# Second cross attention: an item's key scales are issued ahead of its columns and keys

## The chip, the cores and the metric

The kernel runs on one core of a Trainium2 chip. The metric is the device time of one execution in microseconds (us). The engines named here are TensorE (PE in the profile; PEld is its weight load), VectorE (DVE), ScalarE (ACT), GpSimd (POOL) and SyncE (SP), which here only waits and issues DMAs.

## The reference, cut to what matters

The model is two layers of cross attention, self attention and a routed feed-forward part on x of 64 x 32 x 256, with a context of 64 batch items of 257 keys and 128 features. The change lies in the cross attention of the second layer:

```
def _L1_xattn_ref(hidden_states, encoder_hidden_states, Wq, Wk, Wv, Wo, gq, gk):
    q = (hidden_states @ Wq).reshape(B, Sq, H, D)           # H = 16 heads, D = 128
    k = (encoder_hidden_states @ Wk).reshape(B, Skv, H, D)
    v = (encoder_hidden_states @ Wv).reshape(B, Skv, H, D)
    q = rmsnorm(q, gq)
    k = rmsnorm(k, gk)
    scores = jnp.einsum('bqhd,bkhd->bhqk', q, k) * scale
    attn = jax.nn.softmax(scores, axis=-1)
    out = jnp.einsum('bhqk,bkhd->bqhd', attn, v)
    return out.reshape(B, Sq, H * D) @ Wo
```

The key weights are folded into the queries ahead of time, so the scores come straight from the context. What is left of the key's rmsnorm is one factor for each head and key, 1 / rms(k), by which a score is multiplied before the softmax.

## The kernel before, in words

`cross_attention` (from L380) is used for both layers; everything below holds for layer 1, the second. An item is one batch element. `ITERS` = 8 passes handle `NB` = 8 items each; the document counts passes and the items of a pass from 0. An item has 16 heads of 32 queries, that is 512 rows of scores, or R = 4 tiles of 128 rows by 257 keys. So a pass has ST = 32 tiles, 0 to 31, and tile 4b is the first of item b.

For each item three things come from DRAM. The *pair* (L534) holds the item's columns (the context transposed, which the scores read) and its keys (which the mixing reads), in one transfer of 256.5 KB into one of RING = 8 places. The *key scales* (L539) hold the factors 1 / rms(k) for all heads, spread over the partitions that hold a head's 32 queries, in HR = 4 transfers of 128.5 KB into one of SCALES = 4 places; the trace calls them all_big<-rk, as the places lie in a large shared buffer. Nothing else in the item loop is loaded by SyncE, but for the weight codes of the next stage (`load_codes`, L2185) behind items 1 and 3 in passes 0 to 3, and its scales (`load_scales`, L2195) ahead of the last pass. GpSimd gathers rows of the expert output for the next pass by its own DMAs (L1065), 2 to an item in passes 0 to 5, each item's behind the mixing of an earlier one.

The work on a tile s: TensorE computes the scores (`score`, L604 to L614, into one of two PSUM buffers); VectorE multiplies them by the key scales and takes each row's maximum (`weigh`, L857), which frees the PSUM buffer; VectorE makes the shift (L865), ScalarE the exponential (L747), VectorE the division (L881); TensorE turns the tile (`turn`, L620), ScalarE keeps it (L755), and TensorE mixes it with the keys (`mix`, L634). On TensorE a step s of a pass is turn(s), score(s + AHEAD), mix(s - LAG), with AHEAD = 6 and LAG = 3. Behind step 31 come the head of the next pass (query norms L577, queries L600) and the projection (L643), between which the first 6 scores of the next pass stand. All engines work in program order.

Who waits for the loads: the score of an item's first tile waits for the pair (`keys_loaded`), the weighing of its first tile waits for the key scales (`kscale_loaded`). Score s also waits until tile s - 2 is weighed. SyncE waits, ahead of a pair, until the item 8 before it is mixed (`mixed`), and ahead of the key scales until the item 4 before it is weighed (`weighed`). Both counters start with a credit, of RING and of PRE = 12, so that the first places count as free:

```
pe.sem_inc(mixed, RING)
dve.sem_inc(weighed, PRE)
```

SyncE calls `items` for passes 0 to 3, then in a loop for passes 4 to 6, waits for the query norms of the last pass (`n_made`), loads the scales of the next stage, and calls `items` for pass 7.

Of the kernel before, what the change touches and what calls it, by code (L numbers as in the profile page):

```python
# [379 lines left out]
def cross_attention(nc, I, layer, x_sb, ident, ctxT, folded, spare, rk_dram, last_cols, pairs, slots_all=None,  # L380
# [7 lines left out]
    with ExitStack() as ctx:  # L388
# [9 lines left out]
        RING, SCALES = (8, 4) if layer else (4, 2)  # L398
# [20 lines left out]
        else:  # L419
            pair = sc.sb("pair", [P, RING, PAIR])  # L420
# [35 lines left out]
        keys_loaded = [sc.sem(f"keys_loaded{n}") for n in range(RING if layer else ROWS)]  # L456
# [14 lines left out]
        mixed = sc.sem("mixed")  # L471
# [5 lines left out]
        def _(sp):  # L477
            sc.clear_next(sp)
            if layer == 0:
# [24 lines left out]
                with sp.Fori(0, ITERS - 1) as i:  # L504
                    for b in range(NB):
                        item = i * NB + b
# [23 lines left out]
            def items(i, codes=False):  # L530
                for b in range(NB):
                    item = i * NB + b
                    sp.wait_ge(mixed, item + 1)
                    sp.dma_start(pair[:, b % RING, :], pairs[bass.ds(item, 1), :, :].rearrange("a p n -> p (a n)")  # L534
                                 ).then_inc(keys_loaded[b % RING], 16)
                    sp.wait_ge(weighed, item * R)
                    for j in range(HR):
                        src = rk_dram[bass.ds(item, 1), :, j * R:(j + 1) * R, :].rearrange("a c r s -> (a c) (r s)")
                        sp.dma_start(key_scale[j * T:(j + 1) * T, b % SCALES, :, :].rearrange("p r s -> p (r s)"),  # L539
                                     src.unsqueeze(1).broadcast_to([RK_COPIES, T // RK_COPIES, R * S2])  # L540
                                     ).then_inc(kscale_loaded[b % SCALES], 16)
                    if codes and b in (1, 3):
                        after.load_codes(sp, ("wq", "wk")[b // 2], i, codes_ahead)

            for g in range(SA_GROUPS):
                items(g, codes=True)
            with sp.Fori(SA_GROUPS, ITERS - 1) as i:
                items(i)
            sp.wait_ge(n_made, ITERS * (G * NQ))
            for m in range(SCALE_SLOTS):  # L550
                after.load_scales(sp, m, scales_ahead)
            items(ITERS - 1)
            sp.wait_ge(weighed, ITERS * ST + PRE)
            for g in range(SA_GROUPS):
# [2636 lines left out]
```

## Time and profile before

| | |
|---|---|
| median of 3 runs | 2654.81 us (2651.01 to 2657.32) |
| the profiled execution | 2667.95 us, span 2666.0 us |
| granted TensorE clock, mean | 0.983 of full speed |
| PE busy | 2538.4 us, 95% of the span |
| DVE, ACT, POOL busy | 51%, 48%, 29% |
| DMA, mean | 73 GB/s; the queue of SyncE 20.6% of 16 engines, POOL's 5.3% |

The second cross attention takes the span from 1269 to about 1930 us, its passes start some 80 us apart. Busy means that an engine executes; semaphores, branches and the issue of DMAs are not counted. A releaser (behind "<-") is the instruction or the transfer that ended the idle time before an instruction.

### The profile page before, as it was taken

To read this page: it belongs to the slowest core of one execution; us is meant where nothing else is said; L and a number is where in the kernel's file an instruction comes from. 1 tells how busy PE (TensorE), PEld (TensorE's weight loads), DVE (VectorE), ACT (ScalarE), POOL (GpSimd) and SP (SyncE) were. 2 spreads that over 40 slices of the span, in tenths; PEclk is the share of its full clock that TensorE was granted. 3 is DMA by queue.
4 is the path that set the end of the run, shared out by engine and by line. 5 is a ranking of instruction groups with operands and counts; after the bars stand their busy time and mean duration, and the time that the engine had idled before them with its cause. 6 is when DMAs were issued, how large, how long until landed. Compare 5 with 4: busy or idle time off the path is not lost. (4 is left out here: it accounts for less than half of the span.)

```text
span 2666.0 us, 56230 instructions
## 1 busy us (share of the span) xinstructions
PE 2538.4 (95%) x16582; PEld 1904.6 (71%) x16582; DVE 1350.9 (51%) x4801; ACT 1269.6 (48%) x5190; POOL 769.3 (29%) x979
## 2 busy tenths in 40 slices
PE   7999999999999999998899999999879999999888
PEld 6888888878544444445677777777768888888777
DVE  3555555546677754446434455444424444444434
ACT  2555555544466666665545665556412222222142
POOL 1332232347355520003424323231061111111132
PEclk9999999999899999999999999999989999999999
DMA  6222222110510024422534543333380000000033
GB/s 191 71 63 65 66 64 66 53 46 0 167 48 2 1 72 134 128 58 62 145 103 125 138 111 93 85 100 89 107 205 5 8 8 8 5 7 8 8 92 122
DMA packets 176273, 195.16 MB, mean 73 GB/s; under 512 B 39993, under 2 KB 141687, under 8 KB 175378
## 3 DMA queue, kind: packets, MB, share of 16 engines
q1 hardware_dynamic: 146146, 157.65, 20.6%
q0 software_dynamic: 17744, 32.60, 5.3%
q10 hardware_dynamic: 12256, 3.44, 0.8%
q8 instruction: 52, 0.85, 0.1%
q14 instruction: 75, 0.61, 0.1%
HBM read 150.44 MB, written 56.62 MB: 78 GB/s over the span
## 5 line engine op out<-in xcount | busy, mean ns | idle before, releaser
L2326 PE MATMUL sa_work_ps<-sa_xnT,all_big 128*128 128x128 f32 x2048 | 243.0, 281 | 18.1 <-POOL all_big L2661 6.6
L2326 PEld LDWEIGHTS sa_work_ps<-sa_xnT,all_big 128*128 128x128 f32 x2048 | 237.7, 196 | 22.2 <-POOL all_big L2661 6.9
L267 PE MATMUL rt_kn_key_ps<-moe_w_wk,all_big 128*128 128x512 f32 x560 | 250.4, 600 | 0.8 <-DVE moe_kn_stats L316 0.4
L755 ACT ACTIVATE xa_probsT<-xa_probsT_ps 128x256 f32<-128x256 f32 x512 | 190.9, 374 | 98.0 <-PE xa_probsT_ps L620 91.5
L600 PE MATMUL xa_misc_ps<-xa_xnT,cross_folded 128*128 128x256 f32 x1024 | 233.4, 382 | 0.7 <-ACT xa_xnT L721 0.7
L643 PE MATMUL xa_misc_ps<-cross_folded,xa_mixT 128*128 128x256 f32 x1024 | 229.3, 379 | 0.0
L600 PEld LDWEIGHTS xa_misc_ps<-xa_xnT,cross_folded 128*128 128x128 f32 x1024 | 196.4, 192 | 31.7 <-ACT xa_misc_ps L730 3.3
L2419 ACT ACTIVATE sa_kT<-sa_work_ps,sa_bias_k 128x128 f32<-128x128 f32 x256 | 73.0, 368 | 302.9 <-PE sa_work_ps L2326 302.9
L643 PEld LDWEIGHTS xa_misc_ps<-cross_folded,xa_mixT 128*128 128x128 f32 x1024 | 194.6, 190 | 26.5
L620 PE MATMUL xa_probsT_ps<-all_ident,xa_probs 128*128 128x128 f32 x1024 | 198.0, 275 | 4.7 <-DVE xa_probs L881 3.9
L747 ACT ACTIVATE xa_probs<-xa_probs,xa_shift,xa_row_scale 128x257 f32<-128x257 f32 x256 | 152.6, 596 | 89.9 <-DVE xa_shift L865 89.8
L267 PEld LDWEIGHTS rt_kn_key_ps<-moe_w_wk,all_big 128*128 128x128 f32 x560 | 104.8, 192 | 120.8 <-issue 114.5
L881 DVE TENSOR_SCALAR xa_probs<-xa_probs,xa_share 128x257 f32<-128x257 f32 x512 | 183.3, 380 | 13.6
L288 ACT ACTIVATE rt_kn_key_ps<-rt_kn_key_ps 128x128 f32<-128x128 f32 x560 | 148.3, 265 | 85.1 <-PE rt_kn_key_ps L267 85.1
L267 PE MATMUL ex_kn_key_ps<-moe_w_wk,all_big 128*128 128x512 f32 x400 | 181.3, 597 | 0.7 <-DVE moe_kn_stats L316 0.7
L747 ACT ACTIVATE xa_probs<-xa_probs,xa_top 128x257 f32<-128x257 f32 x256 | 129.9, 507 | 108.0 <-DVE xa_top L857 106.0
L620 PEld LDWEIGHTS xa_probsT_ps<-all_ident,xa_probs 128*128 128x128 f32 x1024 | 140.7, 142 | 56.8 <-DVE xa_probs L881 9.9
L613 PE MATMUL xa_score_ps<-xa_pair,xa_qT 128*128 128x257 f32 x512 | 155.7, 394 | 22.1 <-DVE xa_top L857 21.1
L1065 POOL DMA_INDIRECT all_big<-slot_out,xa_places x104 | 105.8, 1017 | 204.0 <-PE xa_mix_ps L634 179.4
L857 DVE CUSTOM_DVE_ANT_0 xa_probs<-xa_score_ps,all_big 128x257 f32<-128x257 f32 x256 | 105.9, 423 | 108.1 <-PE xa_score_ps L613 67.0
L634 PE MATMUL xa_mix_ps<-xa_probsT,xa_pair 128*128 128x256 f32 x512 | 155.1, 386 | 0.0
L1703 POOL DMA_INDIRECT slot_rows<-rt_xn,rt_places x128 | 126.3, 987 | 99.7 <-DVE rt_places L1634 52.0
(395 smaller groups left out, 5025.8 us busy)
## 6 DMA issues: line engine op xcount, KB each, us to landing
all_big<-rk SPq DMA_DIRECT2D x256, 128.5 KB
xa_pair<-pairs SPq DMA_DIRECT2D x64, 256.5 KB, 14.8
pairs<-all_big SPq DMA_DIRECT2D x64, 128.5 KB, 3.1
moe_w_wk<-in_ctx_dram SPq DMA_DIRECT2D x64, 128.0 KB, 2.5
pairs<-xa_keys SPq DMA_DIRECT2D x64, 128.0 KB, 2.1
cross_folded<-in_L_ffn_w_gate_dram SPq DMA_DIRECT2D x32, 192.0 KB, 2.6
cross_folded<-in_L_ffn_w_up_dram SPq DMA_DIRECT2D x32, 192.0 KB, 2.7
ff_rows<-pairs SPq DMA_DIRECT2D x35, 128.0 KB, 2.1
```

The costliest lines, as they stand in the source:

```text
L267: pe.matmul(self.key_ps[m % self.banks][0:n, :], self.ctxT[:, c * P:c * P + n], self.wk[:, q * 512:(q + 1) * 512], start=True, stop=True). ...
L288: ins = act.activation(keys, keys, ACT.Square, accum_out=self.sums[0:n, c, h * self.NQ + q:h * self.NQ + q + 1])
L600: ins = pe.matmul(misc_ps[hp % 2][:, j * N:(j + 1) * N], folded[:, 2 * hp + j, c * P:(c + 1) * P], xnT[:, c, :], start=(c == 0), stop=(c = ...
L613: pe.matmul(score_ps[s % 2][:, 0:S2], qT[:, b, r * HR:(r + 1) * HR, :].rearrange("p h t -> p (h t)"), columns[:, b % RING, :] if layer els ...
L620: ins = pe.transpose(probsT_ps[s % 2][:, k * P:(k + 1) * P], probs[:, s % SR, k * P:(k + 1) * P], ident[:, :])
L634: ins = pe.matmul(mix_ps[b % 2][:, cols], keys[:, b % RING, k, :], probsT[:, b % 2, k, cols], start=(k == 0), stop=(k == KB - 1))
L643: ins = pe.matmul(misc_ps[t][:, 0:D], mixT[:, h, t * P:(t + 1) * P], folded[:, h, NC * P:FOLDED], start=(h == 0), stop=(h == H - 1))
L747: act.activation(probs[:, s % SR, :], probs[:, s % SR, :], ACT.Exp, bias=least, scale=scale, accum_out=total[:, col]).then_inc(exped, 1)
L755: act.activation(probsT[:, b % 2, :, r * P:(r + 1) * P], probsT_ps[s % 2][:, 0:KB * P].rearrange("p (k n) -> p k n", k=KB), ACT.Copy).then ...
L881: dve.tensor_scalar(probs[:, s % SR, :], probs[:, s % SR, :], share[:, s % SR:s % SR + 1], None, ALU.mult).then_inc(probs_ready, 1)
L1703: pool.indirect_dma_start(out=slot_rows, out_offset=bass.IndirectOffsetOnAxis(ap=places[:, n % 2, k:k + 1], axis=0), in_=xn[:, n % RING, : ...
L2326: ins = pe.matmul(ps[:, j, :], w[:, c, h * HD:(h + 1) * HD], xnT[:, c, :], start=(c == 0), stop=(c == NC - 1))
```

## The change

Two statements of `items`, the wait on `mixed` and the transfer of the pair, move behind the wait on `weighed` and the four transfers of the key scales. They stay ahead of the load of codes. Nothing else differs.

```diff
             def items(i, codes=False):
                 for b in range(NB):
                     item = i * NB + b
-                    sp.wait_ge(mixed, item + 1)
-                    sp.dma_start(pair[:, b % RING, :], pairs[bass.ds(item, 1), :, :].rearrange("a p n -> p (a n)")
-                                 ).then_inc(keys_loaded[b % RING], 16)
                     sp.wait_ge(weighed, item * R)
                     for j in range(HR):
                         src = rk_dram[bass.ds(item, 1), :, j * R:(j + 1) * R, :].rearrange("a c r s -> (a c) (r s)")
                         sp.dma_start(key_scale[j * T:(j + 1) * T, b % SCALES, :, :].rearrange("p r s -> p (r s)"),
                                      src.unsqueeze(1).broadcast_to([RK_COPIES, T // RK_COPIES, R * S2])
                                      ).then_inc(kscale_loaded[b % SCALES], 16)
+                    sp.wait_ge(mixed, item + 1)
+                    sp.dma_start(pair[:, b % RING, :], pairs[bass.ds(item, 1), :, :].rearrange("a p n -> p (a n)")
+                                 ).then_inc(keys_loaded[b % RING], 16)
                     if codes and b in (1, 3):
                         after.load_codes(sp, ("wq", "wk")[b // 2], i, codes_ahead)
```

## Rows read from the trace of the kernel before

**Rows 1.** Busy time by stretch; the first line names the columns, the second is pass 4.
```profile
core 0: us, PE busy (x) PEld busy (x) DVE busy (x) ACT busy (x) POOL busy (x), PEclk, DMA share, GB/s
1630.00:1712.00 82.00, 79.42 (x358) 61.82 (x357) 38.20 (x158) 46.77 (x173) 27.30 (x37) 0.98 0.39 103
```

**Rows 2.** Waits, 1260 to 1930: who, for whom, us in total, times, longest.
```profile
PE xa_score_ps L613 <- DVE xa_top L857: 21.1, 18, 3.1
DVE xa_probs L857 <- DMA all_big<-rk: 20.4, 11, 3.0
...
SPq L539 <- DVE xa_top L857: 245.3, 32, 34.7
```

**Rows 3.** VectorE in order of time: start, us, instruction [idle before <-releaser]; passes 4, 7, 7.
```profile
1665.17 0.43 DVE L857 CUSTOM_DVE_ANT_0 xa_probs<-xa_score_ps,all_big 128x257 f32<-128x257 f32 x1 [2.15 <-DMA all_big<-rk]
...
1887.91 0.42 DVE L857 CUSTOM_DVE_ANT_0 xa_probs<-xa_score_ps,all_big 128x257 f32<-128x257 f32 x1 [0.54 <-DMA all_big<-rk]
...
1906.44 0.43 DVE L857 CUSTOM_DVE_ANT_0 xa_probs<-xa_score_ps,all_big 128x257 f32<-128x257 f32 x1 [1.62 <-DMA all_big<-rk]
```

**Rows 4.** TensorE in order of time, scores: passes 1, 4 (three), 5 (two), 6, 7.
```profile
1420.63 0.70 PE L613 MATMUL xa_score_ps<-xa_pair,xa_qT 128*128 128x257 f32 x2 [2.16 <-DVE xa_top L857]
...
1661.10 0.60 PE L613 MATMUL xa_score_ps<-xa_pair,xa_qT 128*128 128x257 f32 x2
...
1662.19 0.60 PE L613 MATMUL xa_score_ps<-xa_pair,xa_qT 128*128 128x257 f32 x2
...
1665.66 0.99 PE L613 MATMUL xa_score_ps<-xa_pair,xa_qT 128*128 128x257 f32 x2 [2.22 <-DVE xa_top L857]
...
1743.06 0.60 PE L613 MATMUL xa_score_ps<-xa_pair,xa_qT 128*128 128x257 f32 x2
...
1746.33 0.70 PE L613 MATMUL xa_score_ps<-xa_pair,xa_qT 128*128 128x257 f32 x2 [0.93 <-DVE xa_top L857]
...
1821.88 0.60 PE L613 MATMUL xa_score_ps<-xa_pair,xa_qT 128*128 128x257 f32 x2
...
1906.93 0.70 PE L613 MATMUL xa_score_ps<-xa_pair,xa_qT 128*128 128x257 f32 x2 [1.11 <-DVE xa_top L857]
```

**Rows 5.** DMA issues: out<-in, engine, count, KB each, median us to landing.
```profile
all_big<-rk SPq DMA_DIRECT2D x256, 128.5 KB
xa_pair<-pairs SPq DMA_DIRECT2D x64, 256.5 KB, 14.8
```

**Rows 6.** SyncE's issues in order of time, pass 4: scales 4, pair 5, scales 5, 9.
```profile
1630.22 3.30 SPq L539 DMA_DIRECT2D all_big<-rk  x4
1633.78 0.34 SPq L534 DMA_DIRECT2D xa_pair<-pairs  x1
1639.30 3.30 SPq L539 DMA_DIRECT2D all_big<-rk  x4
...
1656.56 6.11 SPq L539 DMA_DIRECT2D all_big<-rk  x4
```

**Rows 7.** Line 534, issue to landing: pairs of 1633.78; 1655.83; 1867.82 and 1874.03.
```profile
DMA to landing us min/median/max: 5.3/5.3/5.3
...
DMA to landing us min/median/max: 16.8/16.8/16.8
...
DMA to landing us min/median/max: 14.6/14.6/14.6
```

**Rows 8.** Busy time by stretch: a pause, the end of pass 6's loads, scales in pass 7.
```profile
1690.00:1706.00 16.00, 16.00 (x76) 14.09 (x75) 9.09 (x20) 2.37 (x5) 9.22 (x18) 1.00 0.01 3
...
1821.00:1824.00 3.00, 3.00 (x18) 2.53 (x16) 2.52 (x13) 3.00 (x10) 0.00 (x0) 1.00 0.02 8
...
1897.00:1900.00 3.00, 2.52 (x15) 1.97 (x13) 1.24 (x6) 2.81 (x10) 0.00 (x0) 1.00 0.25 102
```

**Rows 9.** Busy time by stretch of 1 us, after the stalls of passes 1, 4.
```profile
1422.00:1423.00 1.00, 1.00 (x7) 0.85 (x7) 0.71 (x4) 1.00 (x3) 0.00 (x0) 1.00 0.96 228
...
1666.00:1667.00 1.00, 1.00 (x4) 0.80 (x3) 0.86 (x5) 0.70 (x3) 0.00 (x0) 0.50 0.57 148
```

## The prediction

> **What bounds the kernel now.** I read the busy time by pass first, then the waits, then the order of time on VectorE, TensorE and SyncE. The second cross attention has eight passes of 8 items; an item is four score tiles, so a pass has tiles 0 to 31. TensorE is busy for 79.42 us of the 82 of pass 4 [rows 1]: it is the bound, and a delay counts only where it stops TensorE. VectorE waits 11 times, 20.4 us in all, for the transfer of the key scales (all_big<-rk), and TensorE 18 times, 21.1 us, for VectorE behind it [rows 2]. SyncE waits 245.3 us for scale places to be weighed out [rows 2]: that wait, not the one on "mixed", sets its timing.
>
> The stall comes once a pass, at the last item. In pass 4 VectorE resumes at 1665.17 [rows 3] for tile 28, the first of item 7. TensorE may be two tiles ahead: it had done scores 28 and 29 at 1661.10 and 1662.19 and stands idle for 2.22 us before score 30 [rows 4]. The same shape is in passes 1 to 5, in pass 0 for items 6 and 7, not in pass 6, and in pass 7 for its last four items.
>
> **What the queue does.** An item's key scales are 4 transfers of 128.5 KB, its pair (columns and keys) is one of 256.5 KB [rows 5]. In pass 7, which has no gathers, the pairs issued at 1867.82 and 1874.03 both land 14.6 us later [rows 7], at 1882.4 and 1888.6. So an item takes 6.2 us of the queue, against 4 steps of 1.09 us on TensorE (the distance of scores 28 and 29 [rows 4]). The scales issued just ahead of the second of these pairs let VectorE go at 1887.91 [rows 3]: the pair is down 0.7 us behind them, and the scales take 6.2 - 0.7 = 5.5. While scales move, the DMA share is 0.25, at 102 GB/s [rows 8]: they keep a part of the DMA engines busy, and what the pair has there waits behind them.
>
> **The change, part by part.** Nothing is added or removed: per item one wait on "mixed", one on "weighed", four scale DMAs, one pair DMA, 64 times. The order (mixed, pair, weighed, scales) becomes (weighed, scales, mixed, pair).
>
> *SyncE.* Scales of item n may go when item n-4 is weighed (4 places), a pair when item n-8 is mixed (8 places). Tiles are weighed 6 ahead of the turns and mixed 3 behind them, so "mixed" for item n comes true 4 x 4 - 9 = 7 tiles before "weighed" for n. Hence scales leave when they did. Before, pair 5 leaves right behind scales 4 (1633.78 behind 1630.22) and then SyncE pauses to 1639.30 [rows 6]; after, pair 4 leaves there. The stream of scales and pairs in turn stays, with every pair one item later. Behind the moved "mixed" wait stand its pair, at items 1 and 3 of four passes a load of codes, and the next scales; none is held, as the wait is already true. SyncE's issue time is unchanged.
>
> *The scales gain nothing in passes 0 to 5.* After each pause the queue is empty (share 0.01 over 16 us [rows 8]). Ahead of scales 7 stood scales 4 to 6 and pairs 5 to 7, now scales 4 to 6 and pairs 4 to 6: as many bytes. VectorE's 1665.17 would be possible as before.
>
> *The pairs lose their lead.* Score 28 needs pair 7, which now lands behind scales 7. Behind means 0.7 us in pass 7; with gathers, the pair issued at 1655.83 lands 16.8 us later [rows 7], at 1672.6, so a pair, scales and a pair take 7.5 us from 1665.17, and (7.5 - 5.5) / 2 = 1.0. I take 0.8. With D for VectorE's old resumption, score 28 starts at D + 0.8 and score 30 two steps later, at D + 0.8 + 2.17 = D + 2.97; before, it starts at 1665.66, which is D + 0.49 [rows 3, 4]. That is 2.5 us a pass. The other pairs: pair 4 enters an empty queue, where one landed in 5.3 us [rows 7]; pair 6 may be 1 or 2 us late, but this idle time is part of the wait for pair 7, whose landing the queue sets, and isn't counted again. Six passes: 15.0 us.
>
> *Pass 6* has no gathers. Its queue is empty from 1821 on (share 0.02 [rows 8]), so scales 7 end there and pair 7 would at 1821.7, just before score 28 at 1821.88 [rows 4]. 0 us; at worst 1.
>
> *Pass 7* starts behind SyncE's long wait for the query norms, pair 0 first. After, scales 0 go first; up to item 7 it is the same set of bytes, so pair 7 lands when scales 7 did. VectorE's 1906.44 [rows 3], less 0.1, becomes the start of score 28, and score 30 comes at 1908.5 where it was at 1906.93 [rows 4]: 1.6 us. A stall at its early items is taken up, as its end is set by the queue.
>
> *TensorE's clock.* After the 2.22 us of idle time in pass 4 the granted clock is 0.50 [rows 9], and a tile's score takes 0.99 us, no longer 0.60 [rows 4]. It lasts some 3.5 us, at half speed 1.8 us lost. Passes 0, 2 and 3 pay the same already. Pass 1 (2.16 us idle [rows 4], then 1.00 [rows 9]), pass 5 (0.93) and pass 7 (1.11) don't. The idle time now reaches from where score 28 stood to D + 0.8, in pass 5 from 1743.06 to about 1746.6 [rows 4]: 3.5 us. I count a fall for passes 1 and 5, 3.6 us. Bounds: none anew, 0; or three passes and a second fall at item 6 in each of six, 9 x 1.8 = 16.
>
> **Sum.** 15.0 + 0 + 1.6 + 3.6 = 20.2 us. The profiled execution took 2667.95 us (2666.0 of span, 1.95 around it), 13.1 above the median of 2654.81; it would take 2688, and the median 2675.0.
>
> **A rule to weigh.** A pair lands 0.7 us behind the scales issued before it [rows 3, 7]. The Trainium skill ("DMA: Bandwidth & Descriptors", Queues, rings and completion order) says that copies of one issuing engine need not complete in the order of issue, and that a copy may run on fewer than the sixteen engines. If that let the pair by, the change would be nearly free; the trace agrees with the few engines (share 0.25), and shows no pair overtaking. What it would give is the first rival.
>
> **Rivals.** (1) *The pair passes the scales on the queue*, and is down in the 5.3 us of a near-empty one. Pair 7, issued at about 1651, lands by 1657, ahead of 1661.10; TensorE stands as before, and pass 7 gains the pair that no longer leads its scales, 0.7 us: 2654, not slower. It decides where pair 7 lands 4 us (1665.17 - 1661.10) or more ahead of its scales. Against it: 14.6 and 16.8 us wherever the queue is loaded. (2) *Late pairs cost more than one stall a pass*: a pair takes 1.6 us between gathers, and the clock falls twice: 6 x (2.5 + 0.8) + 1.6 + 16 = 37.4, time 2692. For it: one landing stretches from 14.6 to 16.8 us with the gathers. (3) *The stall pays for itself in part*: a TensorE that stops at score 24 or 28 sends POOL's gathers later, off the time of scales 7, which land 1.2 us sooner, and the clock doesn't fall anew: 6 x (2.5 - 1.2) + 1.6 = 9.4, time 2664. (4) *The order on SyncE doesn't reach the queue*, because SyncE is held by a full ring: its issue of four scales stretches from 3.30 to 6.11 us [rows 6]; but only behind scales 7. Then 0, 2655.
>
> **Chances.** Forecast (14 to 28 us) 0.55; rival 2, 0.12; rival 3 (6 to 14 us) 0.18; rivals 1 and 4, 0.15. Of the last, 0.11 lies within 0.2% (5.3 us, about what a measurement of this kernel can tell from no change) and 0.04 is faster by more, as no row shows where more than 5 us would come from. Slower by over 0.2%: 0.85. The range of 2656 to 2691 leaves about 0.1 below and 0.07 above.
>
> **What would show it.** Right: SyncE's scales at the same distances, each followed by its own pair; VectorE's waits for the rk transfer gone or near zero; in passes 0 to 5 TensorE idle for 3 to 5 us before the first score of item 7, not the third, and score 30 about 3 us behind where scales 7 land; pairs in a loaded queue down 14 to 17 us after their issue; pass 6 as long as before. Wrong: VectorE still waiting for rk, TensorE idle for under 3 us at item 7, or a time under 2659.

## The result and the profile after

The changed kernel takes 2672.65 us (median of 6 runs, 2668.57 to 2675.06), the kernel before 2650.65 us (6 runs, three of them those known at the forecast). The medians are 22.0 us apart; the measured ratio is 1.0073, 95% interval 1.006 to 1.0085, which is 15.9 to 22.5 us. Forecast were 2675.0 us, and 20.2 us more than the 2654.81 us of the runs known then.

The waits of the second cross attention after the change, longest first (who, for whom: us in total, times, longest):

```profile
DVE xa_probs L857 <- PE xa_score_ps L613: 84.2, 65, 4.6
...
PE xa_score_ps L613 <- DMA xa_pair<-pairs: 27.7, 17, 4.0
...
PEld xa_score_ps L613 <- DVE xa_top L857: 5.7, 13, 1.2
```

VectorE's wait for the rk transfer ([rows 2]: 20.4 us) is gone. In its place TensorE waits for the pair itself, 27.7 us in 17 waits, which answers to its 21.1 us behind VectorE in [rows 2]. SyncE's issues in pass 4 answer to [rows 6] (start, us):

```profile
1631.73 3.29 SPq L536 DMA_DIRECT2D all_big<-rk  x4
1635.28 0.34 SPq L540 DMA_DIRECT2D xa_pair<-pairs  x1
1640.81 3.29 SPq L536 DMA_DIRECT2D all_big<-rk  x4
```

Scales 4 and scales 5 are 9.08 us apart, as before (1630.22 and 1639.30), and the transfer behind scales 4 is now pair 4, no longer pair 5. TensorE's scores in order of time, pass 4, answer to [rows 4]:

```profile
1658.11 0.67 PE L613 MATMUL xa_score_ps<-xa_pair,xa_qT 128*128 128x257 f32 x2 [0.53 <-DMA xa_pair<-pairs]
...
1665.62 1.20 PE L613 MATMUL xa_score_ps<-xa_pair,xa_qT 128*128 128x257 f32 x2 [2.86 <-DMA xa_pair<-pairs]
...
1667.89 1.06 PE L613 MATMUL xa_score_ps<-xa_pair,xa_qT 128*128 128x257 f32 x2
...
1670.03 1.06 PE L613 MATMUL xa_score_ps<-xa_pair,xa_qT 128*128 128x257 f32 x2
```

The stall stands before tile 24 (item 6) and tile 28 (item 7), the first tiles of their items. Before the change it stood before tile 30, because VectorE was the one that waited. Tile 28 is scored at 1665.62 and tile 30 at 1670.03, at half clock (the matmuls take 1.06 us in place of 0.60), where tile 30 had gone at 1665.66 with scales 5 issued 1.5 us earlier.

The two first traces show less than the runs: the second cross attention takes 8.5 us more (667.5 and 659.0, counted here and below from the first transposition, L568, to the start of the last addition, L887), and the rest 6.0 us less. The trace of before had longer stalls in this stage than two later traces of the same order; experiments 1 and 2 show them.

### The profile page after: what moved, and what is told of

The parts are those of the page before. It is cut to its first block and busy times, and to the rows that moved or that the text cites. A ratio compares the mean times of both kernels' runs of the same rounds, so it can differ in the third digit from the quotient of the medians.

```text
span 2668.5 us, 56230 instructions
## 1 busy us (share of the span) xinstructions
PE 2538.2 (95%) x16582; PEld 1909.8 (72%) x16582; DVE 1352.4 (51%) x4801; ACT 1268.4 (48%) x5190; POOL 769.8 (29%) x979
## 5 line engine op out<-in xcount | busy, mean ns | idle before, releaser
L2326 PEld LDWEIGHTS sa_work_ps<-sa_xnT,all_big 128*128 128x128 f32 x2048 | 236.4, 196 | 20.8 <-POOL all_big L2661 6.7
L613 PE MATMUL xa_score_ps<-xa_pair,xa_qT 128*128 128x257 f32 x512 | 158.8, 401 | 29.8 <-DMA xa_pair<-pairs 27.7
L613 PE MATMUL xa_score_ps<-all_big,all_spare 128*128 (+1 forms) x512 | 154.5, 389 | 1.3 <-DVE xa_any_key L964 0.9
```

What stands on the lines that cost most here:

```text
L613: pe.matmul(score_ps[s % 2][:, 0:S2], qT[:, b, r * HR:(r + 1) * HR, :].rearrange("p h t -> p (h t)"), columns[:, b % RING, :] if layer els ...
L2326: ins = pe.matmul(ps[:, j, :], w[:, c, h * HD:(h + 1) * HD], xnT[:, c, :], start=(c == 0), stop=(c == NC - 1))
```

## The experiments

The runs came in three groups, each with its own runs of the kernel before, whose median differs by up to 1.5% from group to group (2683.82 for experiments 1 and 2, 2692.53 for 4 and for the first two kernels of 5, 2653.09 for 3 and the last of 5). Microseconds behind a ratio are the ratio less 1, times the median of the kernel before in that group.

**1. The kernel before once more, and the changed kernel beside it.** No edit.

> The kernel before, unchanged, as a control and for a second trace of it: its first trace took 2667.95 us where its median is 2650.65. Ratio 1.000 within 0.002. Theory (queue): in the new trace VectorE waits for the rk transfer once a pass at item 7, 0.9 to 3 us; the 17 us that the first trace took over the median lie in granted clock and in other stages, so that the second cross attention is 5 to 12 us shorter than the 659.0 us (1269.7 to 1928.7) of the first trace. Rival: the first trace is typical, the stage takes 659 +- 1 again, and the changed kernel loses its time in a stage outside the change.

> The changed kernel, unchanged, next to the same runs of the kernel before. Ratio 1.007 to 1.009. TensorE waits for the pair at items 6 and 7 of passes 1 to 5, together 3 to 4 us a pass; second cross attention 668 +- 2 us.

Measured: 0.9998 (0.9985 to 1.0011) for the kernel before, and 1.0062 (1.0045 to 1.0079), 16.6 us, for the changed one, a little under the 1.007 to 1.009 expected. Busy time by pass of the new trace of before; the stretches run from scales 4 of a pass to scales 4 of the next, passes 0, 1, 3 and 5:

```profile
1336.36:1414.74 78.38, 73.07 (x328) 55.86 (x327) 37.53 (x154) 48.18 (x178) 28.89 (x39) 0.98 0.47 126
1414.74:1493.62 78.88, 77.81 (x357) 60.58 (x357) 38.33 (x156) 46.48 (x173) 27.34 (x37) 1.00 0.46 120
...
1572.37:1651.83 79.46, 77.94 (x358) 60.67 (x358) 38.29 (x157) 46.48 (x173) 27.33 (x37) 1.00 0.41 106
...
1730.49:1809.04 78.55, 77.79 (x358) 60.56 (x357) 38.30 (x157) 46.34 (x173) 25.09 (x34) 1.00 0.37 104
```

and the same of the changed kernel, passes 1, 3 and 5:

```profile
1416.50:1501.71 85.21, 80.37 (x357) 62.69 (x357) 38.46 (x156) 46.85 (x173) 27.42 (x37) 0.96 0.43 111
...
1584.12:1666.52 82.40, 77.94 (x358) 60.63 (x358) 38.46 (x157) 46.65 (x173) 27.45 (x37) 1.00 0.40 102
...
1750.22:1831.55 81.33, 77.81 (x358) 60.55 (x357) 38.46 (x157) 46.44 (x173) 25.14 (x34) 1.00 0.37 100
```

In passes 1 to 5, a pass of before takes 78.6 to 79.5 us (79.1 to 83.0 in its first trace), and the whole stage 646.4 us, not 659: 12.6 us less, just beyond the 5 to 12 us expected. VectorE waits for the rk transfer once a pass at item 7 in passes 1 to 5, as expected, but for 0.3 to 1.1 us, no longer 0.9 to 3. In the stretches where both clocks are 1.00, the change costs 82.40 - 79.46 = 2.9 us and 81.33 - 78.55 = 2.8 us; where the clock falls to 0.96 it costs 6.3. The stage of the changed kernel takes 672.1 us, 25.7 more and 2 over what was expected; the whole execution takes 2700.6 us against 2678.7, so the rest of the kernel took 3.8 us less, for no reason that the runs show. The 25.7 us lie as follows: 1.3 ahead of scales 4 of pass 0, 0.9 from there to pass 1's, 20.8 in passes 1 to 5, 0.2 in pass 6, 2.5 in the rest of the stage, which is mostly pass 7.

**2. Which pass.** The new order in passes 0 to 6 only, and in pass 7 only:

```diff
-                    sp.wait_ge(mixed, item + 1)         # and the pair's transfer
+                    if isinstance(i, int) and i == ITERS - 1:      # second kernel: if not (...)
+                        ...
                     ...
+                    if not (isinstance(i, int) and i == ITERS - 1):    # second kernel: if ...
+                        ...
```

> New order in passes 0 to 6, old order in pass 7 (pair ahead of the scales again). Theory (queue): the loss is 2.5 us in each of passes 0 to 5 and a fall of the clock in two of them, so + 16 to + 21 us against the kernel before, ratio 1.006 to 1.008. Rival (the loss comes in the last pass, whose start waits behind the query norms and whose scales and pairs are issued in one burst): + 0 to + 4, ratio under 1.002.

> Old order in passes 0 to 6, new order in pass 7 alone. Theory (queue): + 1.6 us, as the set of bytes ahead of item 7 is the same and only score 28 comes behind it; ratio 1.0006, within noise. Rival (the loss is in the last pass): + 15 or more, ratio over 1.005.

Measured: 1.0049 (1.0032 to 1.0066), 13.2 us, and 1.0007 (0.9997 to 1.0016), 1.9 us. The first is under the 16 to 21 us expected, though the interval (8.6 to 17.7 us) reaches into it; the second can't be told from nothing. The loss is in the passes before the last, as forecast; the rival is out. In passes 0 to 6 the second kernel has the old order and the first the new one, so their traces are a further pair. Pass 3, old order, then new:

```profile
1569.15:1648.56 79.41, 77.93 (x358) 60.67 (x358) 38.26 (x157) 46.50 (x173) 27.34 (x37) 1.00 0.42 106
...
1580.03:1662.33 82.30, 77.95 (x358) 60.66 (x358) 38.46 (x157) 46.62 (x173) 27.45 (x37) 1.00 0.40 102
```

That is 2.9 us once more; in passes 1 and 4, also at full clock in both, it is 1.3 and 2.5 us. The passes 1 to 5 of this old order take 78.7 to 79.5 us, as in the second trace of before, so it is the first trace that stands apart.

**3. Which item.** In every pass, the new order for items 0 to 6 and the old one for item 7; then the other way round (`if b == NB - 1` before and `if b < NB - 1` behind the scales, and the reverse).

> In every pass the new order for items 0 to 6, the old order for item 7 (its pair leaves directly behind pair 6 and ahead of its own scales). Theory (the queue sets the time at which item 7 is complete, and idle time at item 6 is a part of that same wait): scales 7 land when they did before, TensorE idles 1 to 2 us for pair 6 and less at tile 30, loss 0 to 1 us a pass, + 0 to + 6 us in all. Rival (each late pair costs its own stall, so items 5 and 6 carry their share of the 17 to 22 us): + 8 or more.

> In every pass the old order for items 0 to 6, the new order for item 7 alone: pair 7 behind its scales, pair 6 ahead of its own. Theory: item 7 carries the loss. Up to scales 7 the queue holds one pair less behind the pause (pair 7), so pair 7 lands when scales 7 did, D; score 28 starts at D and score 30 2.17 us later where it was at D + 0.49: + 1.7 us a pass in passes 0 to 5 and 7, + 10 to + 16 us with some falls of the clock. Rival (late pairs of items 4 to 6 matter as much): + 5 or less.

Measured: 1.0006 (0.9993 to 1.0018), 1.6 us, and 1.0063 (1.0051 to 1.0076), 16.7 us, just over the 10 to 16 expected. Item 7 alone carries the loss. TensorE's scores in pass 3 with items 0 to 6 changed (`score` is at L618 here):

```profile
1576.43 0.67 PE L618 MATMUL xa_score_ps<-xa_pair,xa_qT 128*128 128x257 f32 x2 [1.16 <-DMA xa_pair<-pairs]
...
1583.75 0.70 PE L618 MATMUL xa_score_ps<-xa_pair,xa_qT 128*128 128x257 f32 x2 [0.17 <-DVE xa_top L862]
```

and with item 7 alone changed:

```profile
1586.85 1.04 PE L618 MATMUL xa_score_ps<-xa_pair,xa_qT 128*128 128x257 f32 x2 [3.00 <-DMA xa_pair<-pairs]
1588.96 1.07 PE L618 MATMUL xa_score_ps<-xa_pair,xa_qT 128*128 128x257 f32 x2
```

In the first, pair 6 is late by 1.16 us, and next to nothing is left to wait for at item 7 (its VectorE waits for the rk transfer once in the whole stage, 0.27 us in pass 1), where the second trace of before has 1.17 us at item 7 of this pass and 0.16 at item 6: idle time at item 6 is a part of the wait that the queue imposes at item 7, not an addition to it. In the second one wait of 3.00 us stands at item 7, with the slow clock behind it.

**4. The load of the gathers.** In both orders, the gathers for passes 2 to 7 are left out, so VectorE adds rows gathered for pass 1 again; the waits of GpSimd on `gathered` are dropped or shortened with them (not shown):

```diff
-                        gather(range(b * PORTION, (b + 1) * PORTION))
...
-                    dve.wait_ge(gathered, j * (16 * G * K0) + 16 * K0)
+                    dve.wait_ge(gathered, 16 * K0)
```

> Old order; GpSimd's gathers for passes 2 to 7 are left out (VectorE adds rows that were gathered for pass 1 again, so values differ). Theory: an item takes 6.2 us of the queue in place of 7.1, scales 7 land as in pass 6, just in time: no wait for rk in passes 0 to 5, pass 7 as before: - 15 to - 25 us. Rival (the stall does not come from the load on the queue): VectorE still waits 1 to 3 us at item 7.

> New order, with the same gathers left out. Theory (queue): pair 7 lands just in time in passes 0 to 6, so the order costs 0 to 1 us a pass, and 1.6 us in pass 7: + 2 to + 8 us over nog_old. Rival (the order costs the same 2.5 us or more a pass without the load of gathers): + 15 to + 22 us.

Measured against the kernel before: 0.9934 (0.9915 to 0.9953), 17.8 us less, and 0.9979 (0.9968 to 0.9989), 5.7 us less. In the old order VectorE has no wait for the rk transfer left in passes 0 to 6, as forecast. Not all of its 17.8 us are that wait: against the second trace of before the stage is 8.7 us shorter (637.7 us) and what follows it 5.7 us, which the theory does not explain. The new order costs 12.4 us between the medians (2685.99 and 2673.56), more than the 2 to 8 forecast and less than the rival's 15; between the traces of the stage it is 9.3 us (647.0 and 637.7). Of these, passes 1 to 5 give 0.0 to 0.9 us each (78.13 to 78.28 us long in the one, 78.13 to 79.05 in the other), where with the gathers they give 2.8 to 6.3; pass 0 gives 2.5 and 0.8 ahead of its scales 4, pass 6 gives 0.2, and the rest of the stage, mostly pass 7, 3.1. The gathers account for most of the loss in passes 1 to 5, not for that at both ends. The 3.1 us between trace and medians are not explained.

**5. Faster scales.** The same values, read in another pattern, in both orders; the third kernel reads one copy 32 times:

```diff
-                                     src.unsqueeze(1).broadcast_to([RK_COPIES, T // RK_COPIES, R * S2])
+                                     src.unsqueeze(0).broadcast_to([T // RK_COPIES, RK_COPIES, R * S2])   # k8_old, k8_new
+                                     src[j:j + 1, :].broadcast_to([T, R * S2])                            # k32_old
```

> Old order of pair and scales; the scales' transfer reads its source as 8 repeats of the 4 copies instead of 4 copies of 8 repeats, so that the outer dimension of the transfer is 8. All values are the same. Theory (the scales run on a quarter of the DMA engines, and this part sets the queue): the share while scales move goes from 0.25 to 0.5 in pass 7, an item takes 3.4 us of the queue (2.75 + 0.7), less than the 4.35 us of TensorE; VectorE no longer waits for rk, TensorE's 21 us of idle time and about 7 us of half clock go: - 20 to - 28 us, ratio 0.990 to 0.993. Rival (the scales are bound by something else, such as reads of the same DRAM rows): share and time stay.

> New order of pair and scales with the same faster scales. Theory: with 3.4 us of queue for an item there is no stall to lengthen, and the order costs nothing: ratio to k8_old 1.000 within 0.001. Rival (the pair's lateness costs by itself, whatever the queue does): still + 15 us or more over k8_old.

> Old order; each of the four transfers of scales reads one of the four copies 32 times, outer dimension 32, so that it can run on all DMA engines. Theory (engines): an item takes 1.4 + 0.7 = 2.1 us of the queue, but with the outer dimension 8 TensorE has no wait left on it, so the time is that of k8_old, 0.5% under the kernel before, within 0.1%. Rival (32 reads of the same rows of DRAM at once are slow): an item takes longer than with 8 repeats, waits for rk come back.

Measured: 0.9952 (0.9937 to 0.9967), 12.9 us less; 0.9942 (0.9923 to 0.996) in the new order; 0.994 (0.9927 to 0.9952), 2635.05 us against 2653.09, for 32 repeats. DMA issues in the second cross attention (out<-in, count, KB each, median us to landing), first of the kernel before in its second trace:

```profile
xa_pair<-pairs SPq DMA_DIRECT2D x64, 256.5 KB, 14.1
```

with 8 repeats outside, old order:

```profile
xa_pair<-pairs SPq DMA_DIRECT2D x64, 256.5 KB, 3.9
```

and two stretches of its pass 7, while scales and pairs move:

```profile
1911.00:1914.00 3.00, 3.00 (x19) 2.56 (x18) 2.19 (x11) 3.00 (x10) 0.00 (x0) 1.00 0.62 164
1914.00:1917.00 3.00, 3.00 (x18) 2.57 (x17) 2.07 (x12) 2.82 (x10) 0.00 (x0) 1.00 0.52 187
```

The share is 0.52 and more where it was 0.25 [rows 8], 187 GB/s where it was 102. The Trainium skill ("DMA: Bandwidth & Descriptors", Why a DMA increments its semaphore by 16 and not by 1) says that a transfer runs on the largest number of engines up to 16 that divides the slowest dimension of both its sides. By that rule an outer dimension of 4 gives 4 of 16 engines and one of 8 gives 8; the trace agrees, 0.25 and 0.52, though these stretches hold pairs too, so the share of the scales alone isn't shown. For an outer dimension of 32 the rule gives 16; with 32 repeats the share reaches 0.99 in single microseconds of the second half of pass 7, where with 8 it reaches 0.87. With the queue that fast, nothing waits for rk or pairs, passes 1 to 5 take 78.1 to 78.7 us in either order, and the order costs nothing that can be told from noise (the new one is 3.4 us under the old between the medians, and its stage 1.1 us over, 633.5 and 632.4). So a late pair has no price by itself: it has one only where the queue is the last to finish. The gain is 13 us, not the 20 to 28 expected. That expectation came from the first trace, with 21 us of TensorE's waits for VectorE; the second trace has 11.6, and its stage is 14.0 us longer than with 8 repeats, which fits the 13 measured.

## Why the prediction was right

*SyncE's timing* was right: scales at the same distances, each with its own pair, and next to no wait on "mixed" (none among the waits of the first trace after, one of 0.6 us in the second; before it was one of 0.4).

*The scales gain nothing* was right within what the traces can tell. From the issue of scales 5 to the end of the wait at item 7 (VectorE's for scales 7, TensorE's for pair 7) it is, on average over passes 1 to 5, 25.8 us in the first trace of before, 24.4 in the second, 24.8 in the old order of experiment 2; in the new order it is 24.8 in the first trace, 25.1 in the second, 24.8 in experiment 2. So the pair comes when the scales came, give or take 1 us. The 0.8 us by which it should come behind them are not resolved: the traces of one order differ by more, single passes of one trace by 2 us (24.3 to 26.3). The pair of first traces suggested a queue sped up by late gathers (rival 3, 1.2 us a pass); beside the other two of the old order that reading falls.

*The pairs lose their lead*, 2.5 us a pass: measured 2.8, 2.9, 2.9, 2.5 and 1.3 us in the five passes with full clock on both sides (experiments 1 and 2). That item 6 isn't counted again is shown by experiment 3. I named idle times of 3 to 5 us before the first tile of item 7, and under 3 us there as a sign of being wrong. By the letter that sign came true: in passes 1 to 5 of the two traces of the changed kernel it is 1.9 to 2.9 us at item 7. Another 0.5 to 1.9 us stand at item 6, 3.0 to 4.9 us together, so the length was right and its place was not; where item 6 has its old order, experiment 3, the 3.00 us stand at item 7.

*Pass 6*: nothing forecast; its TensorE waited 0.68 us once in experiment 1, its stretch is 61.6 us against 61.4. *Pass 7*: forecast 1.6 us. By the times of experiment 2 it is 1.9, which its interval doesn't tell from nothing; the traces of experiments 1 and 2 give 2.3 to 2.8 us from scales 4 of pass 7 to the end of the stage, so the term was somewhat small. *The start of the stage*: I put nothing ahead of pass 0's scales 4; 1.3 us came there in experiment 1, and 0.2 in experiment 2.

*TensorE's clock* was the term of uncertain size. I counted falls in two further passes, 1 and 5, 3.6 us, against a first trace that already had them in passes 0, 2, 3 and 4. The first trace after has exactly these two more, in passes 1 and 5, and a longer one in pass 4. But how many there are changes from trace to trace. At half clock in passes 0 to 5 the three traces of the old order spend 13.6, 3.4 and 0 us, the three of the new order 23.8, 13.6 and 13.6 us: on average 11.3 us more, of which half is lost, 5.7 us where I had 3.6. The fall behind the stall in pass 5, first trace of the changed kernel, in stretches of 1 us:

```profile
1749.00:1750.00 1.00, 0.64 (x3) 0.62 (x4) 0.40 (x2) 0.00 (x0) 0.00 (x0) 1.00 0.88 189
1750.00:1751.00 1.00, 1.00 (x6) 0.86 (x5) 0.43 (x2) 0.00 (x0) 0.00 (x0) 0.62 0.65 226
1751.00:1752.00 1.00, 1.00 (x3) 0.78 (x3) 0.00 (x0) 0.96 (x3) 0.56 (x1) 0.50 0.24 99
```

TensorE had idled 2.25 us before 1749.36; a microsecond later the granted clock (the figure before the last two) is on its way to 0.50, the lower of its two levels, as forecast for this pass. That behaviour was forecast; its size was an estimate from one trace.

*The sum* came nearer than its terms. In experiment 1 the stage lost 25.7 us, 5.5 more than the 20.2 of the sum, mostly in passes 1 to 5 (20.8 in place of 16.1), and the rest of the kernel took 3.8 us less; against the first trace, from which the sum was worked out, the stage lost only 8.5. The forecast was right because the loss of a pass is a difference, and the longer stalls of the first trace cancel in it; that the total of 20.2 lies so near 22.0 (by the medians), 19.3 (by the first ratio) and 16.6 (in experiment 1) is in part luck.

*The rivals.* The pair does not pass the scales (rival 1): it lands 14 to 19 us after issue wherever the queue is loaded. Two falls in one pass (rival 2) are in none of the three traces: where a pass stands at 0.96, it is one stretch behind item 7's stall that lasts 6.8 us in place of 3.4 (pass 1 of experiment 1: full clock behind the 1.93 us at item 6, half clock from 1451 to 1458). For rival 3 there was only the pair of first traces (see above). Rival 4 is out: the order decides, by 16.7 us for one item of eight.

## What to carry to other kernels

Of two transfers that the same work needs, the one that is awaited first on the engine that bounds should lead on the queue, and moving it behind the other costs its own time plus the work that the engine could have done ahead, here 2.5 to 2.9 us at most stalls (forecast: 0.8 + 1.7, which the runs don't tell apart), with the same bytes on the queue. Test such an order at the item where the queue is deepest; elsewhere it cost nothing that could be measured (1.6 us, interval -1.9 to 4.8, for seven items of eight), and once the queue keeps up (here by a transfer pattern with a larger outer dimension, 0.5 to 0.6% under the kernel before) that holds everywhere. Before explaining a difference of 1% from two traces, take a second trace of the same kernel: here the first lay 17 us over the median of six runs, and its stage 12.6 us over that of the second.

## What the runs showed of the hardware

Reading the same data as 8 x 4 in place of 4 x 8 repeats took the DMA share while scales move from 0.25 to 0.52 and more (pairs included), and a pair's median landing from 14.1 to 3.9 us. Reading one copy 32 times at once was no slower than spreading over four: each transfer of scales lands in 3.9 us, and the stage takes 632.6 us where the 8 repeats take 632.4, in different groups. Idle times of 2.0 to 2.3 us were followed by half clock in some passes and by full clock in others of the same run (2.22 us before 1665.66 and 2.16 us before 1420.63 in [rows 4] and [rows 9]; in the second trace after, 1.91 us before 1535.56 were followed by half clock and 2.22 us before 1618.85 by full clock), so in this kernel the clock could not be forecast from the length of one wait.
